# Self-attention pipelines: the value product moved a turn, a raw copy on ScalarE, a 16-column reciprocal

## What is computed

```python
x = x + L0_attn(LN(x))           # 16 heads of 8, RoPE, causal
x = x + L0_xattn(LN(x), ctx)     # mLSTM
x = x + L0_ffn(LN(x))            # routed experts
x = x + L1_attn(LN(x))           # 16 heads of 8, ALiBi bias, causal
x = x + L1_xattn(ctx, LN(x))     # 8 heads of 64, keys from context and latents
x = x + L1_ffn(LN(x))            # soft experts
# self-attention, per sequence and head:
#   p = exp(q k^T / sqrt(8) + bias - rowmax);  out = (p v) / rowsum(p);  out @ wo
```

## Time and profile before

| | |
|---|---|
| median of three runs | 2278.82 us |
| the profiled execution's own time | 2278.38 us |
| its span, first to last instruction | 2276.6 us |
| mean granted TensorE clock | 0.932 of 2.4 GHz |
| busy: PE, DVE, ACT, POOL | 88%, 70%, 67%, 51% |
| self-attention of layer 0 (first to last, from its first load) | 49 to 276 us |
| self-attention of layer 1 | 985 to 1212 us |
| cross-attention | 1212 to 1546 us |

### The profile page before, as it was taken

One profiled execution on the slowest core, in us unless ns is written; L12 is line 12 of the kernel. 1 busy time (PEld: TensorE's weight loads), 2 busy tenths in 40 slices (PEclk: granted clock), 3 DMA queues, 4 the chain that ended last, 5 costly groups with the idle time before them and its releaser, 6 DMA issues. The chain is left out here.

```text
span 2276.6 us, 62556 instructions
## 1 busy us (share of the span) xinstructions
PE 1997.3 (88%) x23071; PEld 1551.1 (68%) x23164; DVE 1593.3 (70%) x4448; ACT 1525.7 (67%) x4433; POOL 1152.6 (51%) x1476
## 2 busy tenths in 40 slices
PE   4899887638999999969986999986799999999999
PEld 2677653316666666736665888874688888888777
DVE  7688649966666666448884666666777777777667
ACT  4688646638778777849994777774766666666542
POOL 5666325527787878835543223322844545454520
PEclk9999955559999999979998999999899999999999
DMA  3000020021000000000001000001000000000101
GB/s 91 2 2 2 11 34 1 1 57 33 1 1 1 1 1 1 1 10 2 2 2 30 2 2 2 2 2 64 3 5 14 16 5 15 16 3 14 51 3 40
DMA packets 48955, 31.16 MB, mean 14 GB/s; under 512 B 21886, under 2 KB 46350, under 8 KB 48398
## 3 DMA queue, kind: packets, MB, share of 16 engines
q1 hardware_dynamic: 39438, 22.97, 3.6%
q10 hardware_dynamic: 9216, 4.20, 0.7%
HBM read 22.97 MB, written 4.19 MB: 12 GB/s over the span
## 5 line engine op out<-in xcount | busy, mean ns | idle before, releaser
L1026 POOL TENSOR_TENSOR ff_hl<-ff_hid,ff_hh 128x512 fp32r<-128x512 f32 x272 | 354.3, 1311 | 111.2 <-ACT ff_hh L1265 104.9
L1875 POOL TENSOR_TENSOR sm_zsum<-sm_zsum,sm_logits 128x512 f32<-128x512 f32 x120 | 154.6, 1289 | 273.4 <-ACT sm_logits L1901 271.7
L1194 DVE TENSOR_TENSOR ff_hid<-ff_p_b,ff_hid 128x512 f32<-128x512 f32 x240 | 164.2, 685 | 157.7 <-ACT ff_hid L1254 157.3
L1254 ACT ACTIVATE ff_hid<-ff_p_h,ff_b 128x512 f32<-128x512 f32 x272 | 186.0, 684 | 48.2 <-PE ff_p_h L1082 46.8
L1918 ACT ACTIVATE sm_sT<-sm_p_s 128x512 f32<-128x512 f32 x128 | 69.5, 594 | 219.6 <-PE sm_p_s L1711 219.6
L1265 ACT ACTIVATE ff_hh<-ff_hid 128x512 fp32r<-128x512 f32 x272 | 170.2, 626 | 38.7 <-DVE ff_hid L1194 36.4
L543 POOL TENSOR_TENSOR at_kblk<-at_kT,at_heads 128x512 f32<-128x512 f32 x128 | 130.7, 1042 | 106.5 <-PE at_p_s L448 96.9
L1887 POOL TENSOR_TENSOR sm_logits<-sm_logits,sm_peak 128x512 f32<-128x512 f32 x128 | 163.0, 1295 | 12.6 <-ACT sm_comb L1936 11.9
L1725 PE MATMUL sm_p_l<-g_phi,g_xnT 128*128 128x256 f32 x512 | 142.5, 405 | 26.4 <-ACT sm_logits L1946 25.3
L578 ACT ACTIVATE at_pr<-at_p_s,at_small 128x64 f32<-128x64 f32 x512 | 155.5, 336 | 6.7 <-DVE at_small L469 6.5
L1080 PE MATMUL ff_p_h<-ff_xh,ff_w1h 128*128 128x512 f32 x272 | 135.1, 497 | 11.5 <-ACT ff_hid L1254 7.6
(11 more groups left out here) (307 smaller groups left out, 6003.5 us busy)
## 6 DMA issues: line engine op xcount, KB each, us to landing
sm_w<-in_w_soft SPq DMA_DIRECT2D x8, 512.0 KB, 3.3
ff_whole<-in_L_ffn_rW SPq DMA_DIRECT2D x30, 128.0 KB, 2.5
early_xs<-in_x ACTq DMA_DIRECT2D x32, 64.0 KB, 1.9
ld_ctx<-in_ctx ACTq DMA_DIRECT2D x32, 64.0 KB, 2.0
ml_vals<-in_ctx SPq DMA_DIRECT2D x8, 256.0 KB, 4.7
x_kept<-early_xs SPq DMA_DIRECT2D x1, 2048.0 KB, 8.2
g_xnT<-x_kept SPq DMA_DIRECT2D x1, 2048.0 KB, 7.8
out_x<-sm_acc SPq DMA_DIRECT2D x8, 256.0 KB, 2.3
```

The costliest lines, as they stand in the source:

```text
L1026: eng.tensor_tensor(hl[:, q, :], hid[:, q, :], hh[:, q, :].bitcast(F32), ALU.subtract).then_inc(h_split, 1)
L1194: dve.tensor_tensor(h, p_b[e % 2][:, :], h, ALU.mult).then_inc(scaled, 1)
L1254: act.activation(hid[:, slot(u, c), :], p_h[c % 2][:, :], ACT.Gelu, bias=b1[:, c:c + 1]).then_inc(gelud, 1)
L1875: pool.tensor_tensor(z, z, logits[:, j % RING_L, :, :], ALU.add).then_inc(summed, 1)
```

## The change

In both self-attentions:

- PE transposes tile t (before: t-1) first, then makes the value product of t-1 at once; the reciprocals turned are those of t, and this product stands behind the value projection.
- ACT has all eight exponentials of t+1 first, then the copy of the first transposed bank of t, then a copy `o_raw` of the raw value product of t-1 (in place of `invT`), then the second bank, then the big exponential. `xg` is gone: PE reads `xnT`. Layer 1's copies `qT` and `kT` go to DVE.
- DVE takes the reciprocal on 16 columns and spreads it with a copy (both right behind the sum), then makes `oT` of t-1 from PSUM and `o_raw`, and only then the sum into `x`, the statistics and the RoPE terms. `oT` waits for `o_raw`.

In the cross-attention the transposes stand one step earlier each on PE, and ACT copies the first bank before the values' copies and the second behind them.

```diff
             def turn(t, u):
-                k, v = t - 1, (u - 1) % R
+                k, v = t, u
                 if has(k):
...
+                k, v = t - 1, (u - 1) % R
+                if has(k):
+
+                    pe.wait_ge(v_copied, 2 * (k + 1))
                     if has(k - 1):
                         pe.wait_ge(oT_made, k)
...
+                k, v = t, u
+                if has(k):
+
+
+                    pe.wait_ge(inverted, k + 1)
+                    if has(k - 1):
+                        pe.wait_ge(oT_made, k)
+                    pe.matmul(p_o[:, P:2 * P], inv[:, v % 2, :, :].rearrange("p h d -> p (h d)"), g["ident"][:, :],
+                              start=True, stop=True).then_inc(inv_turned, 1)
...
+                k, v = t, u
+                if has(k):
+
+                    dve.wait_ge(c_exped, k + 1)
+                    dve.tensor_reduce(small[:, v, 1, HH:NH], pr[:, v, half:].rearrange("p (h k) -> p h k", h=HH), AX, ALU.add).then_inc(summed, 1)
+                    dve.wait_ge(summed, k + 1)
+                    if has(k - 2):
+                        dve.wait_ge(inv_turned, k - 1)
+                    dve.reciprocal(small[:, v, 2, :], small[:, v, 1, :]).then_inc(recip, 1)
+                    dve.wait_ge(recip, k + 1)
+                    dve.tensor_copy(inv[:, v % 2, :, :], col_bc(small[:, v, 2, :], HD)).then_inc(inverted, 1)
+                k = t - 1
+                if has(k):
+                    dve.wait_ge(o_copied, k + 1)
+                    dve.wait_ge(inv_turned, k + 1)
+                    if has(k - 2):
+                        dve.wait_ge(y_done, k - 1)
+                    dve.tensor_tensor(oT[:, (u - 1) % 2, :], p_o[:, P:2 * P], o_raw[:, :], ALU.mult).then_inc(oT_made, 1)
                 k = t - 2
...
+                k, v = t + 4, u
+                if not rope and has(k):
+                    dve.wait_ge(qk_done, k + 1)
...
+                    dve.tensor_scalar(qT[:, v, :], p_qk[:, 0:P], float(HD) ** -0.5, None, ALU.mult).then_inc(q_ready, 1)
+                    dve.tensor_copy(kT[:, v, :], p_qk[:, P:2 * P]).then_inc(k_ready, 1)
...
-                turn_copy(t - 1, (u - 1) % 2, 0)
+                k, v = t + 1, (u + 1) % R
+                exps(k, v, range(HH // 2), False)
+                exps(k, v, range(HH // 2, HH), True)
+                turn_copy(t, u % 2, 0)
                 if has(t - 1):
-                    act.wait_ge(inv_turned, t)
+                    act.wait_ge(pv_done, t)
                     if has(t - 2):
                         act.wait_ge(oT_made, t - 1)
-                    act.activation(invT[:, :], p_o[:, P:2 * P], ACT.Copy).then_inc(inv_copied, 1)
...
+                    act.activation(o_raw[:, :], p_o[:, 0:P], ACT.Copy).then_inc(o_copied, 1)
+                turn_copy(t, u % 2, 1)
...
-                    act.activation(xg[:, (u + 1) % R, :], g["xnT"][:, bass.ds(k * P, P)], ACT.Copy).then_inc(xg_copied, 1)
```

The cross-attention's part, on PE and on ACT:

```diff
+                transposes(t, u, 0)
                 if has(k):
                     for b in range(PER):
                         pe.wait_ge(k_lat, 2 * k + b + 1)
...
-                transposes(t, u, 0)
+                transposes(t, u, 1)
                 if has(t + 1):
                     scores(t + 1, (u + 1) % 2)
-                transposes(t, u, 1)
...
+                turn_copy(t, u, 0)
+                if has(k):
                     if has(t - 2):
                         act.wait_ge(pv_done, t - 1)
                     for b in range(PER):
                         act.wait_ge(v_done, PER * k + b + 1)
                         act.activation(vv[:, (u + 2) % 4, b, :], pj[1 + b][:, :], ACT.Copy).then_inc(v_ready, 1)
...
+                turn_copy(t, u, 1)
```

More of the change, by code:

```diff
@@ L327, in attention @@
         pr = m.sb("pr", [P, R, NH * S])
-        small = m.sb("small", [P, R, 2, NH])
-        inv, invT = m.sb("inv", [P, 2, NH, HD]), m.sb("invT", [P, P])
+        small = m.sb("small", [P, R, 3, NH])
+        inv, o_raw = m.sb("inv", [P, 2, NH, HD]), m.sb("o_raw", [P, P])
         pT = m.sb("pT", [P, 2, NH // 2, P])
@@ L339, in attention @@
         summed, inverted, inv_turned = m.sem("summed"), m.sem("inverted"), m.sem("inv_turned")
[L340 removed]
+        o_copied, recip = m.sem("o_copied"), m.sem("recip")
         bv_spread, bv_done, bo_made = m.sem("bv_spread"), m.sem("bv_done"), m.sem("bo_made")
@@ L376, in turn @@
                         mm.then_inc(pt_done, 1)
-                    pe.wait_ge(inverted, k + 1)
+                k, v = t - 1, (u - 1) % R
+                if has(k):
+                    pe.wait_ge(v_copied, 2 * (k + 1))
                     if has(k - 1):
                         pe.wait_ge(oT_made, k)
-                    pe.matmul(p_o[:, P:2 * P], inv[:, v % 2, :, :].rearrange("p h d -> p (h d)"), g["ident"][:, :],
-                              start=True, stop=True).then_inc(inv_turned, 1)
+                    for c in range(4):
+                        if c % 2 == 0:
+                            pe.wait_ge(pt_copied, 2 * k + 1 + c // 2)
+                        for b in range(PER):
+                            for par in range(2):
+                                j = 2 * c + par
+                                at = 16 * (1 - par)
+                                mm = pe.matmul(p_o[32 * c:32 * c + 32, b * S:(b + 1) * S], vblk[:, v, b, j, at:at + 32],
+                                               pT[:, v % 2, j, b * S:(b + 1) * S], start=par == 0, stop=par == 1)
+                    mm.then_inc(pv_done, 1)
                 k = t - 2
@@ L485, in turn @@
                     norm.dve_stats(dve, t - 3, (u - 1) % 2, 1)
[L486 to L490, removed]
                 k, v = t + 4, u % 2
@@ L502, in turn @@
                             row_bc(table[:, i, :], PER), ALU.add, ALU.mult).then_inc(q_terms if i < 2 else k_terms, 1)
[L503 to L514, removed]
+                k, v = t + 4, u
+                if not rope and has(k):
+                    dve.wait_ge(qk_done, k + 1)
+                    if has(k - R):
+                        dve.wait_ge(s_done, k - R + 1)
+                        dve.wait_ge(kblk_ready, k - R + 1)
+                    dve.tensor_scalar(qT[:, v, :], p_qk[:, 0:P], float(HD) ** -0.5, None, ALU.mult).then_inc(q_ready, 1)
+                    dve.tensor_copy(kT[:, v, :], p_qk[:, P:2 * P]).then_inc(k_ready, 1)
                 if has(t - 2):
@@ L595, in turn @@
                     act.activation(pr[:, v, half:], pr[:, v, half:], ACT.Exp).then_inc(c_exped, 1)
[L596 to L603, removed]
                 k, v = t + 2, (u + 2) % R
@@ L1513, in _, with turn_copy @@
                 act.activation(high[:, :], whole[:, :], ACT.Copy).then_inc(w_rounded, 1)
+            def turn_copy(t, u, h):
+                if has(t):
+                    act.wait_ge(pt_done, PER * t + h + 1)
+                    if has(t - 2):
+                        act.wait_ge(pv_done, t - 1)
+                    act.activation(pT[:, u % 2, h].rearrange("p i k -> p (i k)"), p_t[:, :], ACT.Copy).then_inc(pt_copied, 1)
             def exps(k, v, b):
@@ L1542, in turn @@
                         act.activation(vv[:, (u + 2) % 4, b, :], pj[1 + b][:, :], ACT.Copy).then_inc(v_ready, 1)
-                for b in range(PER):
-                    if has(t):
-                        act.wait_ge(pt_done, PER * t + b + 1)
-                        if has(t - 2):
-                            act.wait_ge(pv_done, t - 1)
-                        act.activation(pT[:, u % 2, b].rearrange("p i k -> p (i k)"), p_t[:, :], ACT.Copy).then_inc(pt_copied, 1)
+                turn_copy(t, u, 1)
                 exps(t + 1, (u + 1) % 2, 0)
```

29 lines of the change are left out of this document (3 added, 26 removed).

## The result

| | before | after |
|---|---|---|
| median of four runs each | 2278.36 us (2277.09 to 2283.86) | 2325.07 us (2323.63 to 2328.40) |
| ratio | | 1.0201 (95%: 1.0185 to 1.0218) |
| span of the profiled execution | 2276.6 us | 2324.0 us |
| mean granted TensorE clock | 0.932 | 0.926 |
| busy: PE, DVE, ACT, POOL | 88, 70, 67, 51% | 87, 69, 64, 49% |

What follows compares the result with a forecast made beforehand. The prediction took a circle of waits, no full engine, to bound the self-attentions. 2278.4 + 26.6 (layer 1) + 2.6 (layer 0) - 6 (cross-attention) = 2301.6, forecast 2302 us; own range 2294 to 2310, 8-in-10 range 2284 to 2320.

Steps and rivals of the forecast that it cites:

- The old circle: Self-attentions before the change: a loop of waits through exponentials, scores, transposes and ACT's copy of turned reciprocals, 6.18 us a turn.
- items 1 to 4: Self-attentions: row maxima, eight exponentials, bank copy, then `o_raw` and DVE's wake; 3.86 us from maxima to `oT`.
- item 5: Self-attentions, DVE: from the start of `oT` to the next instruction's start, 0.14 us.
- item 6: Layer 1, DVE: from the sum into `x` to the second normalisation, with waits for POOL, 2.87 us.
- item 7: Layer 1, DVE: from the second normalisation to the next turn's first instruction, 0.26 us.
- Layer 0: Layer 0's self-attention: turn of 6.27 us, +0.09 us for each of 29 turns, +2.6 us in all.
- PE's branch: Layer 0, from `oT` through turned reciprocals to scores: 2.34 us against DVE's 2.41, so 0.2 us more per turn possible.
- Cross-attention: PE's hole moves ahead of the second transposes; 0.20 us less in each of 30 turns, -6 us.
- More is lost: Rival: PE's and DVE's ways meet in layer 0, cross-attention gains nothing, `qT` and `kT` cost time; 2320 us, chance 0.13.
- The first rival: Self-attentions bound by PE's work, some 5.8 us a turn with wakes, not by waits; 2249 us, chance 0.08.
- The clock: Rival: PE granted 1.2 GHz in layer 1, making the turn 11.3 us; 2419 us, chance 0.03.
- Strict order: Self-attentions: DVE and ACT run their queues strictly first-in first-out, so nothing behind `oT` can slip past it.

Runs made afterwards that it cites:

- raw_early: Changed kernel with ACT's raw copy `o_raw` after six exponentials instead of after eight and a bank copy; 2292.04 us.
- wide_recip: Changed kernel with DVE's reciprocal on 128 columns again instead of 16 columns and a spreading copy; 2327.42 us.
- norm1_next: Changed kernel with layer 1's second normalisation moved to the next turn on DVE, just ahead of `oT`; 2288.75 us.
- kblk_late: Changed kernel in which layer 1's POOL waits for DVE's second normalisation before making the block key; 2312.62 us.
- inv_last: Changed kernel with the turned reciprocals placed behind the scores on PE; 2325.73 us.
- oT_late: Changed kernel with `oT` put back on DVE behind the sum into `x`, the statistics and `qT`, `kT` or the RoPE terms; 2368.26 us.

## Why the prediction was wrong in size

- **The old circle cut, a new one closed (items 1 to 4): right.** 3.89 us from maxima to `oT` in both layers, forecast 3.86; `o_raw` was 0.33 and not `invT`'s 0.28. `raw_early` shortens only this term, by 0.75 us, and gains, and `wide_recip` lengthens only what was said to lie beside it and costs nothing.
- **`oT` to the next instruction (item 5): 0.21, not 0.14.** 0.07 x 60 turns, 4 us.
- **Layer 1's wait for POOL (item 6): right**, 2.86 for 2.87 in most steady turns. `norm1_next` takes it away and with the collision gives back 36.7 us.
- **"To the next turn's first instruction: 0.26 us" (item 7): the step that failed.** It was read from the draining turn, in which no tile is left to make a block key for. In steady turns POOL's block key stands at just that place and L274 takes 0.98 instead of 0.34. Measured price: 12 to 14 us (12.4 between the medians, 14.2 in the stage), shown by `kblk_late`; with item 5's 2 us in this layer it is nearly all of the 16.3 us that layer 1's forecast lacks. I had asked for what POOL's late result holds up on DVE, and not what POOL does next, nor what held that back before. The change itself released it: PE was freed, so its scores came early, so POOL's block key no longer waited for them.
- **Layer 0: +7.8 for +2.6.** The turn is 6.42, not 6.27: 0.15 x 29 = 4.4 of the missing 5.2 us, made up of 0.03 (`o_raw`), 0.07 (behind `oT`) and 0.06 (L274 beside POOL's `qT`), less 0.01. With the same code this stage took 232.4 to 234.8 us in the profiles of four kernels, and the difference lies in the filling turns (the first took 6.33 us here and 5.02 in `kblk_late`), so the rest is within its spread. That PE's branch might cost 0.2 more: no, by `inv_last`. The pieces named for that branch add up to 1.91 us and not about 2.0, which makes it 2.28 for 2.34; nothing hung on it.
- **Cross-attention: right**, 5.7 for 6, and by the place of the hole.
- **The rivals.** "More is lost" named none of the true causes, and 2320 was still too low. The first rival's 5.8 us of PE work was read from layer 1's rows; in layer 0 PE alone takes 6.03 us a turn (`raw_early`), so that rival was never within reach there. The clock did fall, but for single turns and not for the stage: 0.93 on average in layer 1, with PE 79% busy; with the collision away, 1.00 gains nothing over 0.94 that the runs show. In the changed kernel itself ten turns have late scores. Eight of them have no collision, at 7.2 to 7.95 us, and two have it, at 8.0 and 8.4; the ten average 7.6 us, less than the 7.85 of the other 17. So on balance the lowered clock didn't lengthen this stage.
- **Strict order.** The forecast read from the earlier trace rows that DVE waits though other work of the turn is ready behind it. The rows don't show that: the next sum needed PE's product, which ended at about 1205.5. The kernel after does show it: in layer 0 PE's product for the sum into `x` (L400) was done at 154.95, and DVE stood idle for 0.67 us until 156.14 because `oT` was ahead of the sum in its queue. The forecast's sums stand.

Not tried: `kblk_late` and `raw_early` together, and two buffers for the turned reciprocals in the one PSUM bank, which would let PE write while ACT and DVE read there unordered.

## What to carry to other kernels

A duration taken from a filling or draining turn is that of an instruction without its neighbours: before using it, list what each other engine will run at that moment in a steady turn, and what has kept it from running there so far. And look in the whole trace for long cases of the same instruction (the least and the most of a tile's view show them), not in the changed stage alone. A change that lets one engine run ahead releases others' work too, and that work may land beside the instruction on which the turn hangs; a wait added off the circle can then be a gain. Before moving an instruction into another's idle time, look up when its own input is made in the new order, not only when its engine is free.

## What the runs showed of the hardware

- **A short VectorE instruction can be held up by a GpSimd one that started just before it.** 128x128 float, SBUF to SBUF, in place of 0.35 us: 0.98 when the 128x512 block key began 0.14 us ahead, and 1.14 and 1.15 in two turns in which the trace puts the block key's start 0.01 to 0.02 us behind it; it ended at 1135.05, just after the first of the two block-key products (1133.93 + 1.04 = 1134.97), and so in all 18 cases. The row maxima that run beside the second one kept their 0.68 us, and the row sums (L482), which read SBUF, took 0.67 to 0.68 us beside a block key and away from one. The Trainium skill ("SBUF — State Buffer", Who interferes with whom) says that VectorE's second pair of ports is shared with GpSimd and locked for a whole instruction, that whoever issues first gets it while the other blocks, that a copy or `tensor_scalar` can want it, and that a `tensor_reduce` on trn2 never contends. The trace agrees on the holding up, on its lasting until the other's instruction ends, and on the reductions; that ports are the cause is the Trainium skill's word and not the trace's.
- **It also goes the other way, a little:** POOL's L263 takes 0.55 us alone and 0.62 where it starts 0.13 us behind the first L274 (1133.34 and 1133.21).
- **A granted clock of 0.93 is an average of two levels.** With PE waiting up to 2.6 us before the turned reciprocals of a turn, it was 0.93 over 140 us: 1.00 in most turns (2.4 GHz), and 0.50 (1.2 GHz) from 1125.00 to 1127.10, after PE had been busy 0.87 of the 3 us before; the scores took 1.98 us there instead of 1.09. In `kblk_late` it was 0.94, and three more products per turn brought it to 1.00.
- **What the lower level costs depends on the circle.** Where the turn hangs on DVE, as in the kernel after, turns with late scores were not longer on average (7.6 and 7.85 us); in `oT_late`, where it hangs on PE, they were (8.2 us, where undisturbed turns take 7.48).
